# A second copy of x for the last addition, its bias added by two accumulating transfers, and the orders of all engines rewritten

## The reference

```python
dg, db = cond @ down_gamma, cond @ down_beta        # per sequence
y = relu(x @ (down_project * dg + db)) @ (up_project * ug + ub) + x
def bitlinear(v, w, b):                             # act_quant: 127 / max|v| per token
    return act_quant(rmsnorm(v)) @ weight_quant(w).T + b   # weights become -1, 0, 1 times mean|w|
out = x + bitlinear(gelu(bitlinear(y, w1, b1)), w2, b2)    # w1: 1024x256, w2: 256x1024
```

## Time and profile before

| what | value |
|---|---|
| median of 3 runs | 87.71 us (87.54 to 88.22) |
| the profiled execution, its own time | 87.23 us |
| its span, first to last instruction | 85.5 us |
| PE busy | 71.1 us, 83% |
| DVE busy | 69.5 us, 81% |
| ACT busy | 65.2 us, 76% |
| POOL busy | 50.9 us, 60% |
| moved by DMA | 9.18 MB |

### The profile page before, as it was taken

One profiled execution on the slowest core, in us unless ns is written; L12 is line 12 of the kernel. 1 busy time (PEld: TensorE's weight loads), 2 busy tenths in 40 slices (PEclk: granted clock), 3 DMA queues, 4 the chain that ended last, 5 costly groups with the idle time before them and its releaser, 6 DMA issues.

```text
span 85.5 us, 1679 instructions
## 1 busy us (share of the span) xinstructions
PE 71.1 (83%) x501; PEld 39.7 (46%) x501; DVE 69.5 (81%) x145; ACT 65.2 (76%) x127; POOL 50.9 (60%) x120
## 2 busy tenths in 40 slices
PE   4985765299999799999999979999775999979740
PEld 1522214124443264367356629566542756666630
DVE  2139289983989999999999997999999399799840
ACT  0601481922999899999999999999799698999600
POOL 6800008830579697698998928964887845505900
PEclk9999759858999999999999999999999999999997
DMA  1997999996000000000110003030003021012033
GB/s 20 293 250 286 420 414 437 429 425 280 15 0 0 0 11 0 8 0 0 67 56 8 0 1 122 0 123 8 0 10 113 0 83 39 0 58 76 0 123 123
DMA packets 3212, 9.18 MB, mean 107 GB/s; under 512 B 370, under 2 KB 882, under 8 KB 2820
## 3 DMA queue, kind: packets, MB, share of 16 engines
q1 hardware_dynamic: 3168, 9.05, 28.1%
q10 hardware_dynamic: 36, 0.04, 0.1%
HBM read 6.98 MB, written 2.10 MB: 106 GB/s over the span
## 4 chain that ended last, share of the span: by engine, by line
PE 40%; DVE 27%; issue 9%; ACT 9%; POOL 6%; DMA 4%; ACTq 1%; DVEq 1%; POOLq 0%
PE out_ps L346 8%; PE up_ps L278 8%; PE h L308 7%; DVE mx L648 5%; PE q2t_ps L332 4%; DMA b1f<-b_rows 4%; DVE q L689 4%; DVE y L733 3%; PE h L315 3%; ACT junk L519 3%; DVE xx L727 3%; POOL q L980 3%; PE h L346 2%; DVE step L657 2%; ACT q2t L546 2%
## 5 line engine op out<-in xcount | busy, mean ns | idle before, releaser
L648 DVE TENSOR_REDUCE mx<-g 128x1 f32<-128x1024 f32 x16 | 19.3, 1210 | 1.0 <-ACT g L511 1.0
L511 ACT ACTIVATE g<-h,deq 128x1024 f32<-128x1024 f32 x16 | 17.9, 1121 | 0.4 <-PE h L315 0.3
L519 ACT ACTIVATE junk<-g,sq_scale 128x1024 bf16<-128x1024 f32 x15 | 17.3, 1162 | 0.0
L308 PE MATMUL h<-w1q,q1t 128*128 128x512 f16 x64 | 16.4, 382 | 0.0
L346 PE MATMUL out_ps<-w2q,q2t 128*128 128x256 f16 x112 | 14.4, 273 | 0.0
L278 PE MATMUL up_ps<-wu,act 128*128 128x512 f32 x16 | 10.4, 740 | 2.6 <-ACT act L472 1.7
L980 POOL TENSOR_SCALAR q<-g,m 128x1024 f32<-128x1024 f32 x7 | 9.4, 1340 | 5.0 <-DVE m L683 5.0
L346 PEld LDWEIGHTS out_ps<-w2q,q2t 128*128 128x128 f16 x112 | 11.0, 98 | 1.6 <-issue 0.3
L332 PE MATMUL q2t_ps<-ident,q 128*128 128x128 f16 x128 | 9.6, 220 | 2.3 <-DVE q L689 2.2
L332 PEld LDWEIGHTS q2t_ps<-ident,q 128*128 128x128 f16 x128 | 7.6, 98 | 6.0 <-DVE q L689 4.1
L987 POOL TENSOR_TENSOR xx<-xx,b 128x512 f32<-128x512 f32 x8 | 10.1, 1278 | 0.1
(11 more groups left out here) (109 smaller groups left out, 115.5 us busy)
## 6 DMA issues: line engine op xcount, KB each, us to landing
xx<-x_both SPq DMA_DIRECT2D x3, 1024.0 KB, 13.2
w<-w_t SPq DMA_DIRECT2D x4, 512.0 KB, 8.7
out<-xx SPq DMA_DIRECT2D x7, 256.0 KB, 2.0
xx<-x_both SPq DMA_DIRECT2D x2, 256.0 KB, 4.5
xx<-x_both SPq DMA_DIRECT2D x1, 512.0 KB, 8.7
upk<-up_pack SPq DMA_DIRECT2D x1, 384.0 KB, 3.6
out<-xx SPq DMA_DIRECT2D x2, 128.0 KB, 1.8
dpk<-down_pack SPq DMA_DIRECT2D x1, 129.0 KB, 2.1
```

The source lines that it names most:

```text
L308: pe.matmul(h[s][:, cols], q1t[:, j % 2, s, c, :], w1q[:, c, cols], start=(c == 0), stop=False)
L511: a.activation(g[:, j % G_RING, s, :], h[s][:, :], ACT.Gelu, scale=deq[:, col:col + 1])\
L519: a.activation(junk[:, j % 2, s, :], g[:, j % G_RING, s, :], ACT.Square, scale=sq_scale[:, 0:1], accum_out=ms[:, col:col + 1]).then_inc(gs ...
L648: v.tensor_reduce(mx[:, col:col + 1], g[:, j % G_RING, s, :], AX.X, ALU.max, apply_absolute_value=True)\
```

## The change

The same work is computed, with five differences.

1. A new tile `xb` holds a second copy of `x`. SP loads it by two transfers of 4 pairs (1 MB each), queued behind all others, in place of the 128 KB of b2.
2. `add_b2` is a transfer that POOL issues: it adds 4 pairs' worth of b2 (now laid out by the host as 128 x 4 x 2 x 256) from HBM onto `xb`. There are two, in place of eight additions on POOL. `combine` reads and writes `xb`, waits for the half's transfer, and the stores read `xb`.
3. `step_of` is a `scalar_tensor_tensor` with the constant tile `over_q` (1/127), in place of a `tensor_scalar`.
4. `square_last` signals a semaphore of its own, `gsq_last`.
5. The lists of calls of PE, ACT, DVE and POOL are written in another order. The two `split_b1` calls, which stood around `scale_down` and `shift_down`, now stand behind `shift_up` and behind `largest_y(1)`.

```diff
-        b2 = sb("b2", [P, D])
+        xb = sb("xb", [P, PAIRS, SLOTS, D])
...
+        over_q = sb("over_q", [P, 4])
...
-            sp.dma_start(b2[:], b2_rows).then_inc(b2_in, 16)
+            for n in range(2):
+                pairs = slice(PAIRS // 2 * n, PAIRS // 2 * (n + 1))
+                sp.dma_start(xb[:, pairs].rearrange("p i s d -> p i (s d)"), x_both[:, pairs, 1]).then_inc(xb_in[n], 16)
...
-                sp.dma_start(out[:, j], xx[:, j, 1]).then_inc(stored, 16)
+                sp.dma_start(out[:, j], xb[:, j].rearrange("p s d -> p (s d)")).then_inc(stored, 16)
...
             def step_of(part, cols):
-                v.tensor_scalar(step[:, cols], mx[:, cols], FLOOR, 1.0 / Q_MAX, ALU.max, ALU.mult)\
-                    .then_inc(step_done[part], 1)
+                v.scalar_tensor_tensor(step[:, cols], mx[:, cols], FLOOR, over_q[:, 0:cols.stop - cols.start],
+                                       ALU.max, ALU.mult).then_inc(step_done[part], 1)
...
             def combine(j, s):
                 col = g_col(j, s)
-                v.wait_ge(xb_ready, j + 1)
+                v.wait_ge(xb_ready[j // (PAIRS // 2)], 16)
...
-                v.scalar_tensor_tensor(x[:, j, s, :], out_bank(j, s), deq[:, col:col + 1], x[:, j, s, :],
+                v.scalar_tensor_tensor(xb[:, j, s, :], out_bank(j, s), deq[:, col:col + 1], xb[:, j, s, :],
                                        ALU.mult, ALU.add).then_inc(out_ready[s], 1)
...
             set_cond()
-            split_b1(0)
             scale_down()
             shift_down()
-            split_b1(1)
             scale_up()
             shift_up()
+            split_b1(0)
             add_x(0)
...
-            def add_b2(j):
-                p.wait_ge(y_ready, j + 1)
-                if j == 0:
-                    p.wait_ge(b2_in, 16)
-                p.tensor_tensor(x[:, j], x[:, j], b2[:, :].unsqueeze(1).broadcast_to([P, SLOTS, D]), ALU.add)\
-                    .then_inc(xb_ready, 1)
+            def add_b2(n):
+                pairs = slice(PAIRS // 2 * n, PAIRS // 2 * (n + 1))
+                p.wait_ge(xb_in[n], 16)
+                p.dma_start(xb[:, pairs], b2_rows, accum_op=ALU.add).then_inc(xb_ready[n], 16)
```

More of the change, by code:

```diff
@@ L366, in _ @@
             weight_sum(0)
+            down(1)
             transpose_q1(0)
-            down(1)
             up(1)
-            keep_busy(2)
+            first_layer(0, 1)
+            transpose_inv(0)
             first_layer(0, 0)
-            transpose_inv(0)
-            weight_sum(1)
[L374 to L379, removed]
+            add_bias(0, 1)
+            down(2)
+            add_bias(0, 0)
@@ L883, in _ @@
-            add_x(4)
-            largest_g(1, 0)
-            largest_g(1, 1)
-            first_steps(1)
-            second_step(1)
-            first_multipliers(1)
+            largest_g(1, 1)
+            largest_g(1, 0)
+            second_step(1)
+            first_steps(1)
+            copy_w2_sums()
+            first_multipliers(1)
+            add_x(4)
+            quantise_first(1)
             second_multiplier(1)
-            quantise_first(1)
-            copy_w2_sums()
+            quantise_y(3)
@@ L892, in _ @@
+            add_x(5)
             largest_y(4)
-            quantise_y(3)
-            largest_g(2, 1)
-            second_step(2)
-            add_x(5)
-            second_multiplier(2)
+            largest_g(2, 0)
             combine(0, 1)
+            first_steps(2)
             combine(0, 0)
-            largest_g(2, 0)
-            first_steps(2)
             first_multipliers(2)
             quantise_first(2)
+            quantise_y(4)
+            largest_g(2, 1)
             largest_y(5)
-            quantise_y(4)
+            combine(1, 0)
@@ L906, in _ @@
+            combine(1, 1)
+            second_step(2)
+            second_multiplier(2)
             largest_g(3, 0)
             first_steps(3)
+            first_multipliers(3)
+            add_x(6)
+            quantise_first(3)
             largest_g(3, 1)
-            add_x(6)
-            first_multipliers(3)
-            combine(1, 1)
-            combine(1, 0)
             second_step(3)
-            quantise_first(3)
+            quantise_y(5)
+            largest_y(6)
             second_multiplier(3)
-            largest_y(6)
@@ L917, in _ @@
-            quantise_y(5)
             largest_g(4, 0)
             combine(2, 0)
+            combine(2, 1)
+            largest_g(4, 1)
             first_steps(4)
+            second_step(4)
             first_multipliers(4)
-            combine(2, 1)
+            second_multiplier(4)
             quantise_first(4)
@@ L1101, in _ @@
             inverse_parts(4)
-            add_b2(4)
-            add_b2(5)
+            quantise_second(2)
             dequantisers(3)
+            quantise_second(3)
             inverse_scale(5)
             inverse_parts(5)
-            quantise_second(3)
-            add_b2(6)
             dequantisers(4)
```

229 lines of the change are left out of this document (115 added, 114 removed).

## The result

The changed kernel takes 92.72 us (median of 4 runs, 91.34 to 93.33) against 87.62 us before. The ratio is 1.0463, with an interval of 1.0332 to 1.0593: clearly slower. (The ratio rests on undisturbed executions alone; of the changed kernel these are the two shorter ones, 91.34 and 92.12 us.) The profiled execution takes 91.34 us, 1.74 us of it around a span of 89.6 us. So the span grew by 4.1 us where I had forecast 2.8 us less.

A forecast was written before the change was run, and what follows sets the result against it. It took PE, DVE and ACT, all full from 30 to 60 us, then a chain, as the bound. Span 85.5 - 2.5 (earlier start) - 0.3 (add_b2) = 82.7 us, + 1.73 + 0.48 = 84.9 us; range 83.2 to 88.3.

The forecast's parts named there:

- the stall of the transfers: DVE's combine waiting for the first accumulating transfer: landing 3.9 us, stall 0; at a quarter rate 12 us, stall 5.6.
- Both move up together, so 6.4 us lie between: First transfer's issue (34.24 us) and combine(0) (40.62) both move earlier together, keeping 6.4 us for landing.
- The second transfer has more than 10 us: Second accumulating transfer: more than 10 us between its issue and the combine that wants it, so no stall.
- Rival 1: Accumulating transfer lands late, combine(0, 1) waits, PE and ACT run dry; decides from 10.1 us landing; 90.5 us, chance 0.16.
- The splits: Start: b1's two splits leave the way to the first y; wu done at 7.8 us, up(0) gains 1.1 us.
- the weights: Start: DVE's share of the sum of |w1| moves up; iws ready at 12.9 us, 1.6 us earlier.
- POOL's chain: Start: POOL's constants and first scales wait for iws, take 5.15 us, end at 18.05, 0.9 us later than before.
- the lead of the first gelu: First gelu at 19.6 us instead of 22.13, so the full stretch starts 2.5 us earlier; bounds 1.5 to 3.3.
- the order of the rest: Calls change places on all engines after the start: counted as 0, with 1.5 us either way.
- Rival 2: Lead at the start doesn't survive: POOL's chain grows beside DVE's rounding, new waits take it back; about 87.5 us, chance 0.18.
- add_b2 leaving POOL: Eight additions, 10.2 us, leave POOL, shortening DVE's steps by 2.3 us; counted as 0.3 us, bounds 0 and 1.4.
- Rival 3: The new two-tensor steps do not wait for POOL, so DVE saves more; 83.5 us, chance 0.14.

The follow-up runs named there:

- e8_first_early: Changed kernel with its first accumulating transfer issued behind inverse_parts(1) and its second behind inverse_parts(2): 84.82 us, ratio 0.9737 to the kernel before.
- e2_nob2: Changed kernel without the two accumulating transfers, so the output lacks b2; combine waits only for the copy of x: 84.41 us, ratio 0.9702.
- e11_first_only: Changed kernel with only its first accumulating transfer moved up, behind inverse_parts(1); the second stays behind inverse_parts(6): 89.47 us, ratio 1.0204.
- e7_new_order_pool: Changed kernel's orders, splits and steps, but b2 added by eight POOL additions as before, without copy or accumulating transfer: 85.53 us, ratio 0.983.
- e12_second_only: Changed kernel with only its second accumulating transfer moved up, behind inverse_parts(3); the first stays behind inverse_parts(2): 88.24 us, ratio 1.007.
- e1_early: Changed kernel with both accumulating transfers issued early, behind inverse_parts(1) and behind dequantisers(0): 86.42 us, ratio 0.9878.
- e4_old_order_xb: Kernel before, old orders, splits and steps, with only the copy of x and two accumulating transfers where add_b2(0) and add_b2(1) stood: 86.97 us, ratio 0.9961.
- e10_plain: Changed kernel with its two transfers at the same places, written plainly to a spare tile without accumulating, so b2 is lacking: 84.36 us, ratio 0.9606.

## Why the prediction was wrong

**The term that failed is the stall of the transfers, "I take 0".** It stood on two numbers, and both were off. The landing was to take 3.9 us, and 7 with twice the data time; it took 8.4 and 7.9. I had doubled the right thing (the data time did double, 5.8 against 2.8 us of the engines), but from too low a base: a plain transfer of this size from POOL's queue takes 5.4 us here, not 3.9. (The Trainium skill, "DMA: Bandwidth & Descriptors", Anatomy of one DMA, has a fit for transfers issued by GpSimd by which this one is estimated at 4.4 us; the plain transfer measured 5.4, and the accumulating one lies at nearly twice the estimate.) My upper bound of 12 us held.

**"Both move up together, so 6.4 us lie between" failed as well.** The combine moved up by 1.6 us, to 38.98, and the issue not at all: inverse_parts(2) was done at 32.62, but POOL idled 1.63 us before the issue at 34.25, which is by chance the time at which add_b2(2) started before (34.24). So 4.7 us lay between, and 8.4 - 4.7 = 3.7 us is the wait that the trace has. Against the 2.5 us to spare in my sum, 4.5 us of the overrun come from the landing and 1.7 from the gap.

**"The second transfer has more than 10 us" was the worst step**, since the prediction has no working for it. The call stands behind inverse_parts(6), where add_b2(7) stood, and even in the kernel before add_b2(7) started at 62.67 us and combine(4) at 68.29, only 5.6 us later. In the new order DVE reaches combine(4) 4.1 us behind the issue. This wait costs 3.1 us of the 6.2.

**Rival 1 was the case, but mis-sized.** Its chain is what happened (DVE stands, behind it the steps and the quantisation, then PE and ACT run dry). But it was given one wait and a threshold of 10.1 us, made of a gap that did not exist, so the time it gave, 90.5 us, was passed with landings of 8.4 and 7.9 us and two waits of less than 4 us each. Its 0.16 was too low for a transfer without any price in the rows.

**The rest of the sum came out near, in part by luck.** The span missed the forecast by 89.6 - 82.7 = 6.9 us. Moving the transfers takes 6.2 of them away: the kernel has then a span of 83.4 us (e8_first_early; 83.1 without any transfer, e2_nob2), 0.7 above my 82.7. The splits, the weights and POOL's chain came within 0.2 us each. But the lead of the first gelu was 1.3 us instead of 2.5 (1.5 in e8_first_early), and what made up for it came from where I had counted 0 or 0.3 us: the order of the rest and add_b2. No run parts these two. In the start I had counted 0.95 us for four products behind transpose_inv(0); PE was at the lower clock (granted 0.50 from 15 to 20 us) and they took 1.91 (18.39 to 20.30). I had seen and used it for the time before, not for my own. In e11_first_only, whose start is the same code, the clock rose about 2 us earlier (0.68 in 18 to 19 us, where the changed kernel has 0.50), the second four products took 1.33 us, and the first gelu started at 19.73. Of the 1.1 us between the two, 0.6 is these products, and 0.4 that POOL's last inv was done at 17.57 instead of 17.93. So the start of one and the same code differs by a microsecond from trace to trace. Rival 2's cause (POOL's chain grows) was not the case, and by e7_new_order_pool the lead survives. (Its time should read 87.7 us: 82.7 + 2.8 + 1.73 + 0.48.)

**add_b2 leaving POOL: little, as counted.** I counted 0.3 us; e2_nob2 against e7_new_order_pool gives 0.7, e8_first_early against it 0.4, and in the old order nothing shows.

**Rival 3 is false.** The two-tensor form waits for POOL: 0.96 and 0.97 us at the same place in either form. (The Trainium skill, "SBUF — State Buffer", Who interferes with whom, states that a DVE instruction with two SBUF inputs contends with a GpSimd instruction that reads SBUF; the trace agrees.)

## What to carry to other kernels

When a transfer takes the place of an instruction, write down for each transfer the time of its issue and the time at which its result is first wanted, both in the new order, and place it where the gap is as wide as your upper bound of the landing. Twice my estimate (7.8 us) would still have been too little for 8.4; the 12 us of the bound would have done, and e8_first_early shows such a place for the first, with 14 us. If there is none, the gain must be larger than the wait. Count the issue as an instruction of the engine that issues it, and look at who waits behind it. And when a change mixes orders with a new mechanism, time each alone: here the orders gained 1.7 us, the mechanism at best 0.7, and its place lost 6.

## What was not expected of the hardware

- An accumulating transfer of 1 MB moves at 131 to 246 GB/s where the plain one has 401 to 459 in its full microseconds, and keeps the DMA engines for twice the time (5.8 us against 2.8). Landing takes 7.9 to 8.7 us in the changed kernel, e8_first_early and e12_second_only, against 5.2 to 5.7; once, in e11_first_only, it took 10.2. Where a second one is issued while the first still moves, it lands later: 10.7 us in e1_early, 12.8 in e4_old_order_xb. Why it is twice the time was not tried: that the destination has to be read as well is an argument, not a measurement.
- POOL idled 1.63 to 1.76 us before the first transfer it issued behind inverse_parts(2), in three kernels (the changed one, e10_plain with 1.69, e12_second_only), though the copy of x had landed at about 27.5 us. The profile names ACT, whose instruction was not what the call waits for. It isn't a price of every first issue: in e4_old_order_xb the first follows the instruction ahead of it (27.33 + 0.23) at 27.61. Nor is it one of the place alone: in e8_first_early the second issue stands there and follows at once (32.79 + 0.23, 33.02). The cause is open.
- The clock can make the effect of a wait last. After the first wait PE's mean granted clock in 40 to 50 us was 0.83 in the changed kernel and in e12_second_only, and 1.00 where the wait was gone. After the second it was 0.84 in 70 to 80 us of e11_first_only, but 1.00 in the changed kernel, though DVE waited as long there (3.86 us against 3.98). So a stall of this length did not cost the clock each time.
